# Attention loop of a two-layer block: the visits in turn, the key projections ahead of the second maximum

## The reference, cut to what matters

```python
qkv = X @ W_qkv
qkv = qkv.reshape(b, s, h, d, 3)
q, k, v = (qkv[..., 0], qkv[..., 1], qkv[..., 2])
scores = jnp.einsum('bqhd,bkhd->bhqk', q, k) / scale
weights = jax.nn.softmax(scores, axis=-1)
attn = jnp.einsum('bhqk,bkhd->bqhd', weights, v)
return attn.reshape(b, s, h * d) @ W_out
```

## Time and profile before

| what | us |
|---|---|
| median of 3 runs | 1828.82 (1826.97 to 1830.44) |
| profiled execution | 1841.47 |
| its span, first to last instruction | 1839.6 |
| TensorE busy in the span | 1727.4 |
| VectorE busy | 1547.9 |
| ScalarE busy | 1459.2 |
| GpSimd busy | 1444.4 |

### The profile page before, as it was taken

One profiled execution on the slowest core, in us unless ns is written; L12 is line 12 of the kernel. 1 busy time (PEld: TensorE's weight loads), 2 busy tenths in 40 slices (PEclk: granted clock), 3 DMA queues, 4 the chain that ended last, 5 costly groups with the idle time before them and its releaser, 6 DMA issues. The chain is left out here.

```text
span 1839.6 us, 32373 instructions
## 1 busy us (share of the span) xinstructions
PE 1727.4 (94%) x9247; PEld 924.8 (50%) x9247; DVE 1547.9 (84%) x2180; ACT 1459.2 (79%) x1954; POOL 1444.4 (79%) x869
## 2 busy tenths in 40 slices
PE   5899999999999999999999999999999899975687
PEld 5444444444444444444444444444444677763456
DVE  7888888888888888888888888888888878888886
ACT  4488888888888888888888888888888777864553
POOL 5388888888888888888888888888888256654664
PEclk9899999999999999999999999999999999997899
DMA  7212121212212121212122121212122777331000
GB/s 258 79 36 80 36 80 46 80 46 69 78 52 86 34 80 36 80 46 80 46 69 82 51 83 34 80 36 80 46 80 62 241 218 218 115 99 48 0 18 29
DMA packets 125334, 143.31 MB, mean 78 GB/s; under 512 B 26737, under 2 KB 106673, under 8 KB 122098
## 3 DMA queue, kind: packets, MB, share of 16 engines
q1 hardware_dynamic: 120306, 132.61, 23.6%
q0 software_dynamic: 4992, 10.27, 1.7%
HBM read 87.20 MB, written 27.64 MB: 62 GB/s over the span
## 5 line engine op out<-in xcount | busy, mean ns | idle before, releaser
L1562 POOL TENSOR_TENSOR psum_k<-psum_k,probs 128x1024 f32<-128x1024 f32 x384 | 929.3, 2420 | 103.9 <-ACT probs L1499 83.8
L1499 ACT ACTIVATE probs<-ps_s 128x1024 f32<-128x1024 f32 x512 | 497.0, 1024 | 149.9 <-PE ps_s L1319 149.9
L1328 PE MATMUL ps_v<-probs,V 128*64 128x512 f32 x2056 | 497.8, 605 | 0.0
L1581 DVE TENSOR_REDUCE mxh<-ps_three 128x2 f32<-128x1024 f32 x264 | 318.5, 1207 | 98.3 <-PE ps_three L1286 98.2
L1483 ACT ACTIVATE ps_s<-peak 128x1024 f32<-128x1024 f32 x224 | 245.1, 1132 | 0.0
L1483 ACT ACTIVATE ps_s<-qkv_raw 128x1024 f32<-128x1024 f32 x224 | 245.0, 1131 | 0.0
L1622 DVE RECIPROCAL e_y_row<-e_y_row 128x128 f32<-128x128 f32 x256 | 241.0, 941 | 0.0
L1328 PEld LDWEIGHTS ps_v<-probs,V 128*64 128x64 f32 x2056 | 124.8, 136 | 228.6 <-issue 209.7
L1319 PE MATMUL ps_s<-e_ew 64*128 64x512 f32 x1536 | 199.0, 391 | 0.0
L1562 POOL TENSOR_TENSOR psum_k<-probs 128x1024 f32<-128x1024 f32 x64 | 152.8, 2388 | 47.2 <-ACT probs L1499 39.4
L854 POOL DMA_INDIRECT results<-e_y_row,e_y_at x92 | 102.6, 1115 | 82.0 <-ACT e_y_row L795 52.8
(11 more groups left out here) (320 smaller groups left out, 3184.4 us busy)
## 6 DMA issues: line engine op xcount, KB each, us to landing
e_ew<-w_split SPq DMA_DIRECT2D x23, 1024.0 KB
qkv_raw<-peaks SPq DMA_DIRECT2D x33, 512.0 KB, 3.9
V<-e_x_raw SPq DMA_DIRECT2D x33, 512.0 KB, 3.6
peak<-peaks SPq DMA_DIRECT2D x32, 512.0 KB, 4.3
xs_hi<-xh SPq DMA_DIRECT2D x16, 512.0 KB, 4.0
xs_lo<-xl SPq DMA_DIRECT2D x16, 512.0 KB, 5.0
rows<-in_blank_d SPq DMA_DIRECT2D x4, 1483.5 KB, 16.9
e_x_raw<-rows SPq DMA_DIRECT2D x23, 258.0 KB
```

The costliest lines, as they stand in the source:

```text
L1328: ins = nc.tensor.matmul(ps_v[rows, :], V[par][:, kt, rows], probs[:, t % RING, x, :], start=kt == 0, stop=kt == KT - 1)
L1499: nc.scalar.activation(probs[:, t % RING, :, :], ps_s[t % 2][:, :, :], ACT.Exp, scale=SCALE).then_inc(p_done, 1)
L1562: nc.gpsimd.tensor_tensor(acc, probs[:, (t - 1) % RING, :, :] if kt == 1 else acc, probs[:, t % RING, :, :], ALU.add).then_inc(add_done, 1)
L1581: nc.vector.tensor_reduce(mxh[:, kh, t, :], max_bank(unit, i)[:, :, :], AX.X, ALU.max).then_inc(m_done, 1)
```

## The change

The visits are put in another order, and all four engines' lists follow it. Before, the order was K1, Q0 with den1, out0, V0, Q1 with den0, out1, V1, K0. After, it is Q0 with den1, out0, K1, V0, then Q1 with den0, out1, K0, V1: visits with the maximum in front and shared ones take turns, and the two halves of a turn are alike. In the visits of keys the projection is issued ahead of the second maximum, in those of queries behind it as before. VectorE's list becomes one function `half`, called twice; its second seed moves from step 13 to step 11; `expert_part` moves from the visit of Q0 to the end of that of K1; `normalise(n, 1)` from the visit of Q1 to the end of that of V0, `normalise(n, 0)` from behind K0's low part to the end of the visit of V1. ScalarE stages the next weights (`stage`) one visit earlier, and GpSimd rounds their low parts two steps earlier.

```diff
-    VISIT = [("K1",), ("Q0", "den1"), ("out0",), ("V0",), ("Q1", "den0"), ("out1",), ("V1",), ("K0",)]
+    VISIT = [("Q0", "den1"), ("out0",), ("K1",), ("V0",), ("Q1", "den0"), ("out1",), ("K0",), ("V1",)]
-    BY_V = (3, 13)
+    BY_V = (3, 11)
...
-                    pe.wait_ge(xv_done, n * PER["v"] + AHEAD["v"])
+                    pe.wait_ge(xa_done, n * PER["a"] + AHEAD["a"])
...
                     if p in SHARED:
                         row_max_shared(n, t, i, other, unit % 2)
+                    elif VISIT[p][0][0] == "K":
+                        item(n, par, VISIT[p][0], b)
+                        row_max(n * 2 + unit, i, other, unit % 2)
                     else:
                         row_max(n * 2 + unit, i, other, unit % 2)
                         item(n, par, VISIT[p][0], b)
...
-                    if p == 5:
+                    if p == VISITS // 2:
                         stage(n)
...
-                    if t != STEPS - 5:
+                    if t != STEPS - 7:
...
+                def half(hf, late, early, par):
+
+                    t = KT - KT * hf
+                    step(t)
+                    step(t + 1)
+                    low(n, early, nxt)
+                    seed(n, t + 3)
+                    row_max_upper(n, t + 2)
+                    row_max_lower(n, t + 2)
+                    row_max_shared(n, t + 3)
+                    inverse(n, hf, 0)
+                    inverse(n, hf, 1)
+                    add_out(n, f"out{1 - hf}")
+                    step(t + 4)
+                    step(t + 5)
+                    low(n, late, par)
+                    inverse(n, hf, 2)
+                    if hf:
+                        expert_part(n)
+                    row_max_upper(n, t + 6)
+                    row_max_lower(n, t + 6)
+                    row_max_shared(n, t + 7)
+                    inverse(n, hf, 3)
+                    normalise(n, hf)
+
+                half(1, "K1", "Q0", nxt)
+                half(0, "K0", "Q1", par)
```

More of the change, by code:

```diff
@@ L1385, in _ @@
                     p = t // 2
-                    b = (n + (2 if p == VISITS - 1 else 1)) // PAIRS % B
+                    b = (n + (2 if VISIT[p][0] == "K0" else 1)) // PAIRS % B
                     unit, i = maximum(t)
@@ L1502, in _ @@
                     if p not in SHARED:
-                        read(n, VISIT[p][0], par if p == VISITS - 1 else 1 - par)
+                        read(n, VISIT[p][0], par if VISIT[p][0] == "K0" else 1 - par)
                     for k in (t + 1, t + 2):
```

## The result

The changed kernel takes 1880.19 us (median of 4 runs, 1878.15 to 1881.11), the kernel before 1827.89 beside it; the ratio is 1.0283, interval 1.0265 to 1.0300. It is slower by 52.3 us, which would be 1.63 us in each of 32 turns. The profiled execution of the changed kernel took 1878.15, with a span of 1876.3.

The account below looks back on a forecast made before the run. TensorE was taken to set the pace; waits hurt only where its next instruction hangs on them. Terms 1.54 + 0.69 − 0.48 − 0.09 − 0.04 − 0.01 = 1.61 us a turn, times 32, gave 1880 us, range 1822 to 1905.

Parts of the forecast that it names:

- The sum: All visits of a turn: 1.61 us more, times 32 turns 51.5 us, on the median of 1828.8 giving 1880 us.
- K1: Visit of keys: projection in front, second maximum at 2.72, visit ends at 5.03, −0.09 us a turn.
- Q0: Visit of queries: first maximum no longer behind other visits' low parts, so 5.89 us as Q1 before, −0.04.
- K0: Visit of keys, likewise with the projection in front: −0.01 us a turn.
- 1893 for the profiled execution: Whole profiled run: the earlier one's 12.7 us surplus over the median was carried over to the forecast.
- V0, the first loss: Experts' part waits for a GpSimd add's end, V0's second maximum starts at 3.42 instead of 1.72: +1.54 us.
- Q1, the second loss: Normalisation waits out an add and ends at 13.05, Q1's second maximum starts at 2.52 instead of 1.83: +0.69 us.
- V1 and the projection in front: V1 lasts 4.85, −0.48, its normalisation ending in time for Q0; in keys' visits the projection exchanges wait for switch.
- the switch: Extra change of matmul shape from the projection in front in keys' visits: estimated 0.10 us, bounds 0 and 0.2.
- Fixed durations: Rival: VectorE operations keep their lengths whatever add runs; turn 0.11 shorter, −4 us, 1825 us; chance 0.09.
- GpSimd between adds: Rival: no add runs when the experts' part comes; −0.76 a turn, −24 us, 1805 us; chance 0.07.
- The normalisation that misses its gap: Rival: V1's normalisation meets the last add, Q0's second maximum at 4.2; +76 us on top, 1956 us; chance 0.10.

Follow-up runs that it names:

- e1: Changed kernel with the experts' part moved to out0's visit, between the first maximum's lower half and the shared maximum: 1800.38 us, ratio 0.9846 to the kernel before.
- e2: Changed kernel with the experts' part in place but its second input read from PSUM, experts' low parts not computed: 1806.75 us, ratio 0.9884.
- e3: Changed kernel with only the normalisation of half 1 moved back into Q1's visit, behind the low part: 1886.75 us, ratio 1.0311.
- e4: e1 with the keys' projection behind the second maximum again: 1829.53 us, ratio 1.0016.
- e5: e1 with one repeated reciprocal (0.86 us) more ahead of each normalisation, past the start of the next add: 2052.90 us, ratio 1.1224.
- e6: e1 with a repeated reciprocal of 48 columns (about 0.35 us) more ahead of each normalisation: 1797.86 us, ratio 0.9836.
- e7: Kernel before with only the keys' projection put in front of the second maximum: 1857.69 us, ratio 1.0165.

## Why the prediction was right

**The sum.** 1880 was forecast and 1880.19 measured. Term by term, from the turns shown (from the first maximum of a visit to the next, against before): V0 +1.62 for +1.54, Q1 +0.67 for +0.69, V1 −0.50 for −0.48, K1 −0.10 for −0.09, Q0 −0.01 for −0.04, K0 0 for −0.01. The two outputs became 0.06 shorter each, which was not forecast and whose cause is open. By the medians a turn is 43.65 against 42.10: +1.55, forecast 1.61. That the total agrees to 0.2 us is luck: V0 is 0.08 longer than forecast, the outputs 0.12 shorter, and one turn has a low clock that costs 1.7 us. The 1893 for the profiled execution did not come true: it took 1878.15; the surplus of the execution before, which lay probably for the most part behind the loop, did not recur.

**V0, the first loss.** Right in place, cause and size: the experts' part begins 5.87 behind K1's first maximum, as forecast, and lasts 1.93 (forecast 1.92); TensorE's second maximum starts 3.51 into V0 (forecast 3.42). e1 and e2 show the cause from two sides. One reading is off, without weight here: 0.28 was taken for the operation's own time, and alone it takes 0.42 (e1), so about 0.14 of it (the difference, an estimate) passes before the add ends.

**Q1, the second loss.** Right: the normalisation lasts 1.86 (forecast 1.85), the second maximum starts at 2.50 (forecast 2.52). e3 shows that it is the normalisation, and that putting it back among the early adds of the half pays nothing; e1 shows that the loss goes with the first.

**V1 and the projection in front.** Right: V1's normalisation began at 4.29 (forecast 4.45) and lasted 1.22 (forecast near 1.0), as it began earlier in the same add; it ended in time for Q0. K1's projection starts at 1.83 (forecast 1.82) and its second maximum at 2.72. The estimated 0.10 for the switch held: 1.83, against the 1.73 at which V1's second maximum starts. That is luck in part: it was read from 0.44 behind a maximum that had waited against 0.36 behind one that had not, and in the changed V0 it is 0.43 behind a maximum that waited, with no projection there (747.68 to 748.11). So that pair need not have shown the switch. That the projection in front merely exchanges a wait for a switch holds for the visits of before; in the new order it is worth 0.53 a visit (e4), because there the wait would be longer. The prediction had said what the part costs, not what it saves.

**The rivals.** Fixed durations are out (e5, e6). GpSimd between adds did not happen by itself; e1 brings it about at another place, with 1800 where the rival reckoned 1805. The normalisation that misses its gap was priced at 76 us for one half; e5 made it happen in both, and the price of the wait was right (157 us for two), but a lower clock came on top that the prediction did not have.

## What to carry to other kernels

In these traces a VectorE `tensor_tensor` with both inputs in SBUF had no fixed length beside GpSimd's adds. Where a kernel has such a pair, ask at which point of which GpSimd instruction it will begin, and place it where GpSimd waits, or take one input from PSUM. In a list written out by hand, read what stands behind a moved instruction up to the next operand that another engine waits for; e7 failed on a seed that stood there. A slack that ends in such a wait is free up to a point and then costs nearly a whole instruction of the other engine (e6 against e5).

## What the hardware showed beyond that

The waiting runs both ways. In the changed kernel GpSimd's add of 746.74 starts while the experts' part still runs, and its record lasts 2.44 instead of 2.38 or 2.39; the adds that start while a normalisation still runs last 2.70 to 2.73 (32 of them). Neither engine shows this as idle time: it lies inside the durations.

TensorE's clock fell in some turns after a wait that it came through in others. Windows view of e3 in one of its six turns of 45.2 us, from V0's start to the end of the wait and from there to the item (columns as above), and TensorE's timeline there:

```profile
176.96:180.50 3.54, 1.90 (x18) 1.25 (x16) 3.54 (x5) 3.00 (x4) 3.38 (x3) 1.00 0.00 0
180.50:184.30 3.80, 3.80 (x11) 0.89 (x11) 2.54 (x3) 1.72 (x2) 3.72 (x2) 0.60 0.31 104
```

```profile
180.49 0.50 PE L1286 MATMUL ps_three<-k_hi,q_hi 64*128 64x512 f32 x2 [1.65 <-DVE mxh L1594]
180.93 3.42 PE L1328 MATMUL ps_v<-probs,V 128*64 128x512 f32 x8
184.28 0.54 PE L1255 MATMUL ps_three<-wv_hi,xs_hi 128*128 x1
```

The engine waited 1.65 us, and the eight matmul records of `values` then took 3.42 instead of the 1.94 of the changed kernel's row of 748.11, which stands behind a wait of 1.59: a mean granted clock of 0.60, so mostly the lower level of 1.2 GHz. In the other turns of e3 and in nearly all of the changed kernel the same wait left the clock alone; in one turn of the changed kernel V0 took 8.38 instead of 6.71, with its second maximum at 3.51 as elsewhere and a granted clock of 0.65 from there to its end. So the length of the single wait does not decide by itself. In e5, with waits near 2.5 us, the low clock came in most visits of queries; one of them, cut at the second maximum:

```profile
785.86:790.20 4.34, 1.87 (x15) 1.25 (x14) 4.26 (x3) 2.91 (x4) 3.54 (x3) 0.95 0.00 0
790.20:797.24 7.04, 7.03 (x18) 2.36 (x19) 3.05 (x3) 2.19 (x3) 2.33 (x2) 0.55 0.03 9
```

A visit of queries whose second maximum starts at 4.3 ends at 8.4 at the full clock (10 of them) and at 9.9 to 11.6 with the low one (53; the first visit of the loop is left aside). What sets the point stays open. It means that a wait of TensorE can cost more than its length, and that the changed kernel, with waits of 1.6 us, paid that in one turn of the loop and e3 in six.
